# Attention with value blocks of two score chunks instead of three, and row-maximum groups issued in pairs at every second block

## The chip, the cores and the metric

The kernel runs on one core of a Trainium2 chip. The metric is the time of one execution on the device in microseconds (us); a time of the kernel is the median of several executions. Engines are named as the profile names them: PE is the TensorE matmul, PEld its weight loads, DVE VectorE, ACT ScalarE, POOL GpSimd and SP SyncE, which here only issues transfers.

## What is computed

One transformer block with adaptive layer norm, on x of shape (2, 2048, 256), in float32:

```python
h = _layernorm(x, axis=-1) * (1 + ca) + sa
x = x + ga * _L0_attn_ref(h, ...)
h = _layernorm(x, axis=-1) * (1 + cb) + sb
x = x + gb * _L0_ffn_ref(h, ...)
```

The attention has 16 heads of size 16. With q = (h W_q + b_q) W_s, k = h W_k + b_k and v = h W_v + b_v, it is softmax(q k^T / 4) v for every head, followed by W_o and b_o. The feed-forward part is a router with 8 experts, each of which takes its best 512 tokens. The change touches only the attention.

## The kernel before

**Stages.** The projections of q, k and v come first (to some 130 us), then the attention loop (to some 1396 us), then the residual and second norm, the selection of tokens, and the experts. All engines run their own programs and meet at semaphores.

**The attention's units.** There are 2 x 16 heads and each is cut into two halves of 1024 queries: 64 units (`UNITS`). A unit has 16 key tiles of 128 (`KT`). For a unit the kernel does three things on PE:

- *Row-maximum groups.* A group (`fill_group`, matmuls on L223) computes scores of 128 queries against 1024 keys into two PSUM banks, with two matmuls of 512 columns, one in the upper 64 rows of the array and one in the lower. DVE reduces each group to maxima (`reduce_group`, L230). A unit has 16 groups. There are two slots of two banks, and `next_group(n)` waits on L1120 until group n - 2 has been reduced. After the first group of the next unit is reduced, DVE joins the 16 results (`join_maxima`, L241 and L247), POOL splits them into a high and a low part (`split_maxima`), and SP carries them through DRAM (L200, then L205) into two extra rows of the queries' operand.
- *Score chunks.* `scores(pe, s, half)` (one matmul of 512 columns on L584) computes 128 keys by 512 queries, with the maximum already subtracted by the extra rows. A unit has 32 chunks. They go through three banks (`SCORE_BANKS`): chunk n waits until chunk n - 3 has been read. ACT takes the exponential of each chunk (L1080) into `pt`. Even chunks use the upper rows of the array and odd ones the lower. The first chunk of a unit waits for the maxima to have landed (L576).
- *Value blocks.* `weigh(block)` multiplies the exponentials of a block of chunks by the values (L1139), into `acc` in bank 7. The output uses 32 columns of the array for each quarter of the queries, so four matmuls run side by side. Each one is float32 and appears as two records. A block waits for its exponentials, and the unit's first block also for ACT to have copied the previous unit's output.

**The order on PE** is written by hand in the loop from L1149. Each round issues the value block that lies `DELAY` = 2 rounds back, then the next score chunks, with groups between them. With `BLOCK` = 3 a unit of 32 chunks has `BLOCKS` = 11 value blocks: a first one of two chunks (`FIRST_BLOCK`) and ten of three. A three-chunk block has eight matmuls: four of 256 columns and four of 128. Every round issues three chunks, or two where b == DELAY, and one or two groups, 16 in the 11 rounds of a unit. Groups run ahead of the scores by some 24 key tiles, so they end before the scores do.

**The order on ACT** is that of the chunks. Before one chunk of each unit it copies the output of the unit before, after all of that unit's value blocks are done:

```python
for n in range(STEPS * 2):
    if n % UNIT_CHUNKS == BLOCK and n > UNIT_CHUNKS:
        take_output(n // UNIT_CHUNKS - 1)
```

where `take_output(u)` waits for `pv_done` of (u + 1) * BLOCKS and makes the copy on L1066. These lines are 1068 to 1070.

**The order on SP** is, for each unit: store the output that ACT has copied, carry the next unit's maxima (`place_maxima`), bring the output into its place, and, after a head's second unit, load the operands of a head to come (`load_next`, twelve transfers, after all scores of the head are issued).

Of the kernel before, what the change touches and what calls it, by code (L numbers as in the profile page):

```python
# [46 lines left out]
UNITS = G * HALVES  # L47
STEPS = UNITS * KT
# [3 lines left out]
AHEAD = KT + LEAD  # L52
EARLY = 3
EARLY_GROUPS = 25
BLOCK = 3
DELAY = 2
UNIT_CHUNKS = 2 * KT
BLOCKS = -(-UNIT_CHUNKS // BLOCK)
FIRST_BLOCK = UNIT_CHUNKS - (BLOCKS - 1) * BLOCK
QB = CH // 4  # L60
# [33 lines left out]
def adaln_moe_block(nc, x, w_q, b_q, w_k, b_k, w_v, b_v, w_o, b_o, w_s, router_w, router_b,  # L94
                    w1, b1, w2, b2, c, w_mod, out):
    ctx = ExitStack()
    with ctx:
# [19 lines left out]
        def bank(i, n=1):  # L117
            return ps[:, i * 512:(i + n) * 512]
# [98 lines left out]
        def fill_group(pe, n, slot):  # L217
            u, k = divmod(n, KT)
            h, f = divmod(u, HALVES)
            r, a, c = h % NBUF, f * (QT // 2) + k // NCH, k % NCH  # L220
            for half in range(2):
                rows = slice(HALF * half, HALF * half + KROWS)
                last = nc.tensor.matmul(slot[:, half * CH:(half + 1) * CH], qp[rows, r, a * P:(a + 1) * P],  # L223
                                        kp[rows, r, c * CH:(c + 1) * CH], start=True, stop=True)
            last.then_inc(groups_full, 1)
# [345 lines left out]
        def scores(pe, s, half):  # L571
            u, kt = divmod(s, KT)
            h, f = divmod(u, HALVES)
            n = s * 2 + half
            if kt == 0 and half == 0:
                pe.wait_ge(maxima_in[u % 2], (u // 2 + 1) * 32)  # L576
            if n == 0:
                pe.wait_ge(minus_in, 16 * 2 * NBUF)
            if n == 2:
                pe.wait_ge(low_done, chunks * 4 - 1)  # L580
            if n >= SCORE_BANKS:
                pe.wait_ge(scores_out, n - SCORE_BANKS + 1)
            rows = slice(HALF * half, HALF * half + MROWS)
            nc.tensor.matmul(bank(n % SCORE_BANKS), kp[rows, h % NBUF, kt * P:(kt + 1) * P],  # L584
                             qp[rows, h % NBUF, f * CH:(f + 1) * CH], start=True, stop=True).then_inc(scores_full, 1)
# [249 lines left out]
        def project_rows(pe, n):  # L835
            if n == 0:
                pe.wait_ge(xb_ready, 2 * NB)
                pe.wait_ge(groups_out, STEPS)
                pe.wait_ge(normalised, G // HG // NB * HALVES)
            if n >= NCH and n % 2 == 0:  # L840
                pe.wait_ge(normalised, (G // HG - 1) * HALVES + (n - NCH) // 2 + 1)
            for half in range(2):
                if n > 0:
                    pe.wait_ge(y_out, n * 2 + half - 1)
                for t in range(2):
                    at = (n % NCH) * CH + (half * 2 + t) * P
                    for k in range(KD):
                        last = nc.tensor.matmul(y_bank(half)[:, t * D:(t + 1) * D], ao[:, n // NCH * KD + k, at:at + P],
                                                wog[:, n // NCH, k, :], start=k == 0, stop=k == KD - 1)
                last.then_inc(y_full, 1)  # L850
# [41 lines left out]
        with nc.Block() as block:  # L892
# [9 lines left out]
            def blocks_until(n):  # L902
                u, c = divmod(n, UNIT_CHUNKS)
                return u * BLOCKS + (c - FIRST_BLOCK) // BLOCK + 2

            def chunks_of(block):
                u, b = divmod(block, BLOCKS)
                end = u * UNIT_CHUNKS + FIRST_BLOCK + b * BLOCK
                return range(end - (BLOCK if b else FIRST_BLOCK), end)

            def group_slot(n):
                return bank(5 - 2 * (n % 2), 2)
# [147 lines left out]
            def _(act):  # L1060
                project_act(act)
                def take_output(u):
                    act.wait_ge(pv_done, (u + 1) * BLOCKS)
                    if u > 1:
                        act.wait_ge(o_stored[u % 2], (u // 2) * 16)
                    nc.scalar.copy(o_sb[:, u % 2, :], acc).then_inc(acc_out, 1)  # L1066
# [4 lines that stand above are left out]
# [35 lines left out]
            @block.tensor  # L1106
            def _(pe):
                project_pe(pe)
                mm = nc.tensor.matmul

                def next_group(n):
                    u, k = divmod(n, KT)
                    h, f = divmod(u, HALVES)
                    r = h % NBUF
                    if f == 0 and k == 0:
                        pe.wait_ge(operands_in[r], (h // NBUF + (r > 0)) * 16 * loads_of_head)
                    if n == EARLY_GROUPS:
                        pe.wait_ge(low_done, chunks * 4)
                        pe.wait_ge(v_out, chunks * 2 - 1)
                    pe.wait_ge(groups_out, n - 1)  # L1120
                    fill_group(pe, n, group_slot(n))

                def weigh(block):
                    u, b = divmod(block, BLOCKS)
                    h = u // HALVES
                    if b == 0:
                        pe.wait_ge(v_staged, h + 1)
                        pe.wait_ge(v_out, chunks * 2)
                        if u > 0:
                            pe.wait_ge(acc_out, u)  # L1130
                    ready = chunks_of(block)
                    pe.wait_ge(scores_out, ready[-1] + 1)
                    for s in sorted({n // 2 for n in ready}):
                        kt = s % KT
                        halves = [n % 2 for n in ready if n // 2 == s]
                        first, many = halves[0], len(halves)
                        probs = pt[:, s % PTS, first * CH:(first + many) * CH].rearrange("p (h t) -> p h t", h=many)
                        for j in range(4):
                            last = mm(acc[32 * j:32 * (j + 1), first * QB:(first + many) * QB], v_st[:, h % NBUF, kt, :],  # L1139
                                      probs[:, :, j * QB:(j + 1) * QB], start=kt == 0, stop=kt == KT - 1)  # L1140
                    last.then_inc(pv_done, 1)

                next_group(EARLY_GROUPS)
                for s in range(1, EARLY):
                    for half in range(2):
                        scores(pe, s, half)
                blocks = UNITS * BLOCKS
                group, chunk = EARLY_GROUPS + 1, 2 * EARLY
                for block in range(DELAY, blocks):  # L1149
                    weigh(block - DELAY)  # L1150
                    b = block % BLOCKS
                    many = FIRST_BLOCK if b == DELAY else BLOCK
                    twice = b != DELAY and (b == 0 or b > DELAY and b % 2 == 1) or block == 2 * DELAY
                    for n in range(many):
                        if n == (0 if twice or b == DELAY else 1) and group < STEPS:
                            next_group(group)
                            group += 1
                        scores(pe, *divmod(chunk, 2))
                        chunk += 1
                    if twice and group < STEPS:  # L1160
                        next_group(group)
                        group += 1
                    if block == blocks - DELAY:
                        project_rows(pe, 0)
                for block in range(blocks - DELAY, blocks):
                    weigh(block)
                post_pe(pe)
# [629 lines left out]
```

## Time and profile before

| what | value |
|---|---|
| median of 3 runs | 1736.73 us (1732.57 to 1737.1) |
| profiled execution | 1736.54 us |
| its span (first to last instruction) | 1734.7 us |
| granted TensorE clock, mean | 0.979 |
| attention loop in it | some 139 to 1396 us |
| instructions | 43731 |

The span is what the profile divides into shares; the execution's own time is 1.8 us longer. A group of instructions is one line of the kernel on one engine with one operation. "Busy" is time in which at least one of the group runs, and "idle before" is time in which the engine had nothing just before them, with what ended it. In a timeline, instructions of one line that follow each other are merged, with their count; the first number is the start of the first one in us and the second is the time until the last one ends. Ends of matmuls are modelled and overlap the next start, so costs on PE are read from start to start.

### The profile page before, as it was taken

Reading aid. Unit: us, or ns where it says so; the run is one execution under the profiler, and the core shown is the slowest. Engines: PE = TensorE matmul, PEld = TensorE weight load, DVE = VectorE, ACT = ScalarE, POOL = GpSimd, SP = SyncE. Lnnn points to the kernel's source line nnn. Section 1 sums busy time; section 2 is a strip of 40 time slices with the busy share of each in tenths; the row PEclk is TensorE's granted clock in tenths of the full one; section 3 lists DMA queues with packets and bytes.
Section 4 is the critical chain, followed back from the end, with each engine's and each line's share of the span. In section 5 each row is a group of like instructions: output and inputs, shape, how many; then the busy total and the mean of one; then the engine's idle time right before and its main releaser. Section 6 shows DMA issues by size and latency. Waiting matters only on the chain. (4 is left out here: it accounts for less than half of the span.)

```text
span 1734.7 us, 43731 instructions
## 1 busy us (share of the span) xinstructions
PE 1685.5 (97%) x17251; PEld 969.8 (56%) x17251; DVE 1513.5 (87%) x1908; ACT 1291.7 (74%) x2454; POOL 229.3 (13%) x300
## 2 busy tenths in 40 slices
PE   8999999999999999999999999999999998599998
PEld 5645555555555555555555554555555586488887
DVE  5678999999999999999999999999999476687774
ACT  2327888888888888888888888888888834365663
POOL 0422012100010000001000000100000012135433
PEclk9999999999999999999999999999999997599999
DMA  8660443222222223323222223342220331235332
GB/s 265 207 178 24 92 98 53 41 41 39 52 55 39 41 49 52 47 40 65 41 42 39 39 41 54 59 60 39 41 42 12 108 107 61 98 101 143 89 82 37
DMA packets 93658, 122.03 MB, mean 70 GB/s; under 512 B 24060, under 2 KB 70716, under 8 KB 90348
## 3 DMA queue, kind: packets, MB, share of 16 engines
q1 hardware_dynamic: 84492, 109.22, 28.1%
q0 software_dynamic: 6144, 8.39, 2.7%
q8 instruction: 136, 2.23, 0.6%
q10 hardware_dynamic: 2816, 1.61, 0.3%
q14 instruction: 70, 0.57, 0.1%
HBM read 79.35 MB, written 38.54 MB: 68 GB/s over the span
## 5 line engine op out<-in xcount | busy, mean ns | idle before, releaser
L230 DVE TENSOR_REDUCE pmax<-ps 128x2 f32<-128x1024 f32 x1024 | 1191.6, 1215 | 54.2 <-PE ps L223 50.2
L1080 ACT ACTIVATE pt<-ps 128x512 f32<-128x512 f32 x2048 | 1079.4, 600 | 179.8 <-PE ps L584 157.7
L223 PE MATMUL ps<-kp,qp 48*128 48x512 f32 x2048 | 622.4, 458 | 2.9 <-DVE pmax L230 2.9
L1139 PE MATMUL ps<-pt,v_st 128*32 128x256 f32 (+1 forms) x10752 | 589.7, 334 | 0.7 <-ACT pt L1080 0.7
L584 PE MATMUL ps<-qp,kp 50*128 50x512 f32 x2048 | 560.8, 422 | 0.5 <-ACT pt L1080 0.5
L584 PEld LDWEIGHTS ps<-qp,kp 50*128 50x128 f32 x2048 | 292.5, 185 | 265.2 <-ACT pt L1080 263.1
L1139 PEld LDWEIGHTS ps<-pt,v_st 128*32 128x32 f32 x10752 | 265.7, 109 | 261.0 <-issue 187.2
L223 PEld LDWEIGHTS ps<-kp,qp 48*128 48x128 f32 x2048 | 245.6, 184 | 108.1 <-issue 89.8
L213 POOL CAST m_parts<-rowmax_t 128x32 fp32r<-128x32 f32 x64 | 13.5, 211 | 864.5 <-DVE rowmax_t L247 864.5
L1752 PE MATMUL ps<-w_l,hid_h 128*128 128x256 f32 x256 | 72.3, 283 | 0.0
L446 ACT ACTIVATE pt<-ps,xb 128x512 fp32r<-128x512 f32 x32 | 21.8, 687 | 64.7 <-PE ps L613 63.7
L1518 POOL DMA_INDIRECT y<-b_row,scatter_at x32 | 59.0, 1843 | 35.4 <-DVE b_row L1641 29.0
L613 PE MATMUL ps<-pt,xb 128*128 128x512 f32 x128 | 59.1, 603 | 0.0
L1508 POOL DMA_INDIRECT stage_a<-h_rows,gather_at x32 | 39.0, 1218 | 129.3 <-DVE gather_at L1618 122.0
L1752 PEld LDWEIGHTS ps<-w_l,hid_h 128*128 128x128 f32 x256 | 48.9, 191 | 0.0
L1007 POOL COPY v_st<-v_all 128x256 f32<-128x256 f32 x32 | 12.6, 398 | 260.5 <-PE ps L1139 260.5
L1734 PE MATMUL ps<-qp,kp 128*128 128x512 f32 x128 | 44.3, 428 | 1.4 <-ACT qp L1536 1.2
L1734 PE MATMUL ps<-qp,w_l 128*128 128x512 f32 x128 | 40.2, 396 | 0.0
L1734 PE MATMUL ps<-kp 128*128 128x512 f32 x128 | 40.1, 394 | 0.0
L1536 ACT CAST qp<-ps 128x512 fp32r<-128x512 f32 x16 | 8.6, 590 | 42.0 <-PE ps L1706 42.0
L543 DVE SCALAR_TENSOR_TENSOR pt<-ps,xb,pt 128x512 f32<-128x512 f32 x32 | 23.7, 746 | 17.3 <-ACT pt L446 17.2
L613 PEld LDWEIGHTS ps<-pt,xb 128*128 128x128 f32 x128 | 23.2, 189 | 26.0 <-issue 24.5
(229 smaller groups left out, 1297.6 us busy)
## 6 DMA issues: line engine op xcount, KB each, us to landing
kp<-k_parts SPq DMA_DIRECT2D x186, 128.0 KB, 4.5
v_all<-L_ffn_w SPq DMA_DIRECT2D x16, 1024.0 KB, 6.9
qp<-q_parts SPq DMA_DIRECT2D x186, 64.0 KB, 4.1
k_parts<-pt SPq DMA_DIRECT2D x16, 512.0 KB, 3.4
q_parts<-pt SPq DMA_DIRECT2D x16, 512.0 KB, 2.9
o_rows<-o_sb SPq DMA_DIRECT2D x64, 128.0 KB, 3.4
sums_c<-o_rows SPq DMA_DIRECT2D x512, 0.5 KB
m_rows<-m_parts SPq DMA_DIRECT2D x256, 2.0 KB
```

What stands on the lines that cost most here:

```text
L223: last = nc.tensor.matmul(slot[:, half * CH:(half + 1) * CH], qp[rows, r, a * P:(a + 1) * P], kp[rows, r, c * CH:(c + 1) * CH], start=True ...
L230: v.reduce_max(pmax[:, u % 2, 2 * k:2 * k + 2], slot.rearrange("p (f t) -> p f t", f=2), AX.X).then_inc(groups_out, 1)
L446: nc.scalar.activation(parts[u][:, 0].bitcast(F32R), unit_bank(n, u), ACT.Identity, bias=unit_bias(u)).then_inc(high_done, 1)
L543: v.scalar_tensor_tensor(parts[u][:, 1], unit_bank(n, u), unit_bias(u), parts[u][:, 0], ALU.add, ALU.subtract).then_inc(low_done, 1)
L584: nc.tensor.matmul(bank(n % SCORE_BANKS), kp[rows, h % NBUF, kt * P:(kt + 1) * P], qp[rows, h % NBUF, f * CH:(f + 1) * CH], start=True, st ...
L613: last = mm(unit_bank(n, u), w[:, k, (u % 2) * P:(u % 2 + 1) * P], h_t[n % 2][:, k, :], start=k == 0, stop=k == KD - 1)
L1080: nc.scalar.activation(pt[:, s % PTS, half * CH:(half + 1) * CH], bank(n % SCORE_BANKS), ACT.Exp, scale=SCALE).then_inc(scores_out, 1)
L1139: last = mm(acc[32 * j:32 * (j + 1), first * QB:(first + many) * QB], v_st[:, h % NBUF, kt, :], probs[:, :, j * QB:(j + 1) * QB], start=kt ...
L1508: nc.gpsimd.indirect_dma_start(tok_rows[:, e % 2, cc, :], None, h2_dram, bass.IndirectOffsetOnAxis(ap=gather_at[:, e % 2, cc:cc + 1], axis ...
L1518: nc.gpsimd.indirect_dma_start(out_flat, bass.IndirectOffsetOnAxis(ap=scatter_at[:, e % 2, cc:cc + 1], axis=0), contrib[:, cc, :], None, c ...
L1734: last = mm(bank(2 + f % 2), w[:, k, f * P:(f + 1) * P], t[:, k, :], start=i + k == 0, stop=i + k == KD + 1)
L1752: last = mm(eo_tile(at), h[:, f, tok], w[:, f, :], start=False, stop=f + i == NF + 1)
```

## The change

`BLOCK` goes from 3 to 2. By the formulas that stay, a unit then has `BLOCKS` = 16 value blocks of two chunks, all alike, with four matmuls of 256 columns each. The loop on PE issues one score chunk more before it begins. Each round then issues one value block and two chunks. Rounds with an even number (`pair`) also issue two groups, one before the chunks and one after them; rounds with an odd number issue none. The copy of the output on ACT, whose place is given by `BLOCK`, comes before the third chunk of a unit instead of the fourth.

```diff
--- before.py
+++ after.py
@@ -52,7 +52,7 @@
 AHEAD = KT + LEAD
 EARLY = 3
 EARLY_GROUPS = 25
-BLOCK = 3
+BLOCK = 2
 DELAY = 2
 UNIT_CHUNKS = 2 * KT
 BLOCKS = -(-UNIT_CHUNKS // BLOCK)
@@ -1146,18 +1146,18 @@
                         scores(pe, s, half)
                 blocks = UNITS * BLOCKS
                 group, chunk = EARLY_GROUPS + 1, 2 * EARLY
+                scores(pe, *divmod(chunk, 2))
+                chunk += 1
                 for block in range(DELAY, blocks):
                     weigh(block - DELAY)
-                    b = block % BLOCKS
-                    many = FIRST_BLOCK if b == DELAY else BLOCK
-                    twice = b != DELAY and (b == 0 or b > DELAY and b % 2 == 1) or block == 2 * DELAY
-                    for n in range(many):
-                        if n == (0 if twice or b == DELAY else 1) and group < STEPS:
+                    pair = block % 2 == 0
+                    for n in range(min(BLOCK, UNITS * UNIT_CHUNKS - chunk)):
+                        if n == 0 and pair and group < STEPS:
                             next_group(group)
                             group += 1
                         scores(pe, *divmod(chunk, 2))
                         chunk += 1
-                    if twice and group < STEPS:
+                    if pair and group < STEPS:
                         next_group(group)
                         group += 1
                     if block == blocks - DELAY:
```

## Rows read from the trace of the kernel before

**Rows 1.** The page, part 1: busy us of each engine, share of span, instructions.

```profile
PE 1685.5 (97%) x17251; PEld 969.8 (56%) x17251; DVE 1513.5 (87%) x1908; ACT 1291.7 (74%) x2454; POOL 229.3 (13%) x300
```

**Rows 2.** Instructions grouped by line, 300 to 1300 us: busy, mean ns | idle before.

```profile
L230 DVE TENSOR_REDUCE pmax<-ps 128x2 f32<-128x1024 f32 x815 | 946.9, 1214 | 37.5 <-PE ps L223 34.4
L1080 ACT ACTIVATE pt<-ps 128x512 f32<-128x512 f32 x1629 | 858.9, 600 | 134.5 <-PE ps L584 116.3
L223 PE MATMUL ps<-kp,qp 48*128 48x512 f32 x1628 | 497.7, 457 | 0.5 <-DVE pmax L230 0.5
L1139 PE MATMUL ps<-pt,v_st 128*32 128x256 f32 (+1 forms) x8552 | 469.0, 334 | 0.0
L584 PE MATMUL ps<-qp,kp 50*128 50x512 f32 x1630 | 444.5, 421 | 0.0
L584 PEld LDWEIGHTS ps<-qp,kp 50*128 50x128 f32 x1628 | 232.3, 185 | 210.2 <-ACT pt L1080 210.2
```

**Rows 3.** Line 1066, 300 to 1300 us: count, ns min/median/max, first and last start.

```profile
L1066 ACT COPY o_sb<-ps x51: 389/391/392, 316.4 to 1299.1; 128x256 f32<-128x256 f32 x51
```

**Rows 4.** Timeline of PE, 805 to 812 us: start, us, engine, line, count.

```profile
808.02 0.64 PE L1139 MATMUL ps<-pt,v_st 128*32 128x256 f32 x8
808.59 0.50 PE L223 MATMUL ps<-kp,qp 48*128 48x512 f32 x2
808.93 0.40 PE L584 MATMUL ps<-qp,kp 50*128 50x512 f32 x2
809.26 0.86 PE L1139 MATMUL ps<-pt,v_st 128*32 128x256 f32 x16
```

**Rows 5.** Timeline of PE, 812 to 827 us.

```profile
812.00 0.50 PE L584 MATMUL ps<-qp,kp 50*128 50x512 f32 x1
...
812.34 0.39 PE L584 MATMUL ps<-qp,kp 50*128 50x512 f32 x1
...
812.58 0.41 PE L584 MATMUL ps<-qp,kp 50*128 50x512 f32 x1
812.92 0.86 PE L1139 MATMUL ps<-pt,v_st 128*32 128x256 f32 x16
813.71 0.50 PE L223 MATMUL ps<-kp,qp 48*128 48x512 f32 x2
...
814.89 0.86 PE L1139 MATMUL ps<-pt,v_st 128*32 128x128 f32 x16
815.67 0.50 PE L584 MATMUL ps<-qp,kp 50*128 50x512 f32 x1
...
816.59 0.86 PE L1139 MATMUL ps<-pt,v_st 128*32 128x256 f32 x16
...
825.07 0.66 PE L584 MATMUL ps<-qp,kp 50*128 50x512 f32 x3
```

**Rows 6.** Timeline of DVE, 812 to 824 us.

```profile
816.52 0.18 DVE L241 TENSOR_REDUCE rowmax<-pmax 128x8 f32<-128x32 f32 x1
...
816.87 4.57 DVE L230 TENSOR_REDUCE pmax<-ps 128x2 f32<-128x1024 f32 x4
```

**Rows 7.** Timeline of ACT, 804 to 813 us.

```profile
803.97 1.57 ACT L1080 ACTIVATE pt<-ps 128x512 f32<-128x512 f32 x3
...
807.38 0.39 ACT L1066 COPY o_sb<-ps 128x256 f32<-128x256 f32 x1
807.65 1.60 ACT L1080 ACTIVATE pt<-ps 128x512 f32<-128x512 f32 x3
809.41 1.09 ACT L1080 ACTIVATE pt<-ps 128x512 f32<-128x512 f32 x2 [0.16 <-PE ps L584]
```

**Rows 8.** Timeline of ACT and PEld, 812.5 to 815 us.

```profile
812.60 1.57 ACT L1080 ACTIVATE pt<-ps 128x512 f32<-128x512 f32 x3 [0.15 <-PE ps L584]
...
814.22 0.18 PEld L584 LDWEIGHTS ps<-qp,kp 50*128 50x128 f32 x1 [0.22 <-ACT pt L1080]
```

**Rows 9.** Timeline of PE, 1362 to 1394 us, where the groups have ended.

```profile
1365.26 0.86 PE L1139 MATMUL ps<-pt,v_st 128*32 128x128 f32 x16
...
1367.20 0.86 PE L1139 MATMUL ps<-pt,v_st 128*32 128x256 f32 x16
...
1370.64 0.86 PE L1139 MATMUL ps<-pt,v_st 128*32 128x256 f32 x16
...
1390.59 3.72 PE L848 MATMUL ps<-wog,ao 128*128 128x256 f32 x16
```

**Rows 10.** Timeline of DVE and SP, 834 to 842 us.

```profile
836.16 0.18 DVE L241 TENSOR_REDUCE rowmax<-pmax 128x8 f32<-128x32 f32 x1
...
837.22 1.30 SPq L200 DMA_DIRECT2D m_rows<-m_parts  x4
...
839.42 0.53 SPq L205 DMA_DIRECT2D qp<-m_rows  x2
```

**Rows 11.** Timeline of SP, 816 to 823 us.

```profile
822.35 0.53 SPq L205 DMA_DIRECT2D qp<-m_rows  x2
```

## The prediction

> **What bounds the kernel now.** Four fifths of the span is the attention loop. I read the page first: TensorE (PE) is busy 97%, VectorE (DVE) 87%, ScalarE (ACT) 74% [rows 1]; three engines close to full, so averages do not decide. The grouped rows of the loop's middle say who waits: DVE's reductions sat idle 37.5 us in 1000, nearly all for PE; ACT 134.5 us, for PE; PE's weight loads wait on ACT for 210 us, yet PE has no idle time of its own [rows 2]. One unit (16 groups, 32 score chunks, one output copy) takes (1299.1 - 316.4)/50 = 19.65 us [rows 3].
>
> The timelines then show whether PE is continuous. I measure from the start of one piece to the start of the next. A value block of three chunks holds PE 0.79 us (812.92 to 813.71), the unit's short block of two chunks 0.57 (808.02 to 808.59) [rows 4, 5]. Between value blocks lie 1.18 us with two groups and three chunks (813.71 to 814.89), 0.92 with one group and three chunks (815.67 to 816.59), and 0.67 after the short block (808.59 to 809.26). A unit has 10, 1, 5, 5 and 1 of them: 7.90 + 0.57 + 5.90 + 4.60 + 0.67 = 19.64. That is the whole unit: **PE's issue order is the bound**, and a pause of PE is paid in full. DVE's floor is lower: its reductions start 1.13 us apart when they run back to back (4.57 us for four, the last one 1.22 long [rows 6]), 16 x 1.13 = 18.1 a unit, plus 0.35 for the joining of maxima (816.52 to 816.87) [rows 6]: 18.45.
>
> **Inside a block** the two row halves run together, so matmuls go in slots of two. A slot costs 0.24 (812.34 to 812.58), but the first after a value block 0.34 (808.59 to 808.93, 812.00 to 812.34) and the last before one 0.33 (808.93 to 809.26) [rows 4, 5]. So each edge of a value block costs some 0.10 us, and there will be 16 blocks a unit in place of 11. The Trainium skill ("TensorEngine Tiling (Array Packing)", Key Properties) says that changing the tiling mode drains the array; the value blocks use 32-column tiles and the others do not, so this rule speaks against the change, and the trace agrees with it.
>
> **The change, part by part, against a unit of 19.65.**
> 1. Value blocks: 16 of two chunks at 0.57 = 9.12 (before 8.47): **+0.65**. The same columns are streamed; what is saved is only the third chunk's passes of half width.
> 2. Even blocks: group, two scores, group = three full slots, 0.34 + 0.24 + 0.33, measured 0.92 in the blocks with three slots. Odd blocks: two scores, one slot that has both edges, 0.43: three slots take 0.92 and two 0.67, so one more or less is 0.24 or 0.25. No row shows a slot alone between value blocks; its bounds are 0.33 (one edge free) and 0.50 (the second half late by 0.06, since its bank comes free just then: the score three chunks earlier starts 1.13 earlier, and takes 0.48 to ACT (808.93 to 809.41 [rows 4, 7]), 0.60 there and 0.05 back (814.17 to 814.22 [rows 8])). I take 0.43, nearest to the measured edges. Sum 8 x (0.92 + 0.43) = 10.80 (before 11.17): **-0.37**; full slots are the gain here.
> 3. A pair of blocks is then 0.57 + 0.92 + 0.57 + 0.43 = 2.49 with two groups; DVE needs 2.26. So the DVE gaps grow, and it hides behind PE. Once a unit, the join makes the next reduction start 0.35 late, and the second group of the next even block, whose slot is the one just being read, comes some **0.25** late. Before, DVE was behind by more and PE never waited there.
> 4. **The copy of the output (L1066).** ACT makes it before the exponential of chunk n with n % 32 == BLOCK: third chunk of a unit after, fourth before. It waits for the unit's last value block. After the change this block is issued in iteration 16U+1, behind score chunk 32U+4, and that score waits (three banks) for the exponential of chunk 32U+1. So when ACT has made chunk 32U+1 and comes to the copy, the value block that it wants has by program order not begun. Before, only chunk 32U+2 had to be issued, for which the exponential of 32U-1 is enough: ACT has three exponentials in hand, and the copy starts without idle time (807.38, right behind an exponential [rows 7]). Worked out from the even block's first group at 0: scores 0.34, second group 0.58, last value block 0.91; its matmuls take 0.64 [rows 4] and 0.08 pass to ACT (score ending 809.33, exponential 809.41 [rows 4, 7]): copy at 1.63; exponential 32U+2 at 1.90 (copy to next, 807.38 to 807.65 [rows 7]), ends 2.50. PE meanwhile finished the value block at 1.48 and wants score 32U+5, which waits for exactly this exponential: it starts at 2.55 [rows 8]. Score 32U+6 waits for the next exponential (1.90 + 0.49 + 0.60, spacing from 1.57 us for three [rows 7]), 3.05; the next value block follows 0.34 later at 3.39 and not at 1.91. **+1.48** per unit, 63 times. Behind this wait are queued, on PE, the next value block and the next groups, so DVE starves too; nothing there has slack with which to make it up. Its floor is the wait for the first of these scores alone, 2.55 - 1.48 = 1.07.
>
> Unit: 9.12 + 10.80 + 0.25 + 1.48 = **21.65**, or +2.00. Groups last from block 2 to 998, 997/16 = 62.3 units: +124.6 us. The tail of scores without groups goes by ACT and the three banks: now 3.44 us for six chunks (1367.20 to 1370.64 [rows 9]), 24 blocks at about 1.10 (0.33 + 0.57 + the 0.20 that a bank comes late) = 26.4 for the 25.3 of now (1365.26 to 1390.59), and one more copy: +2.5. One chunk more ahead of the loop waits for an exponential: +0.5. What follows the attention stays: +127.6 in all. The profiled execution took 1736.54, the median of the three runs is 1736.73, no difference, so I forecast **1864 us**.
>
> Costed at nothing: the smaller number of value matmuls (their issue is within the 0.57), the pt slots (twelve chunks, and the values stay within eight of ACT), and **the row maxima**. These must land before a unit's first score. Now this score starts 8.55 us after the join (816.52 to 825.07 [rows 5, 6]); after, groups lead by three pairs of blocks, 7.47 + 0.34 + 0.25 - 1.67 = 6.4 (the score follows the block's first group by 0.34, the join by 0.54 + 1.13). The save is issued 1.06 after the join, the load 3.27 (836.16, 837.22, 839.42 [rows 10]), its second part ends at 3.8; the save, as small, was seen landed 0.9 after its last issue ended (838.52 to 839.42), so the load is there at about 5. That holds, with some 1.4 to spare. In a few units the load comes 5.83 after the join (822.35 [rows 11]), because the next head's operands were still in the queues; those are started at a unit's end, which moves away from the next join by over 3 us.
>
> **The rivals.**
> (a) *Edges are hidden.* The odd blocks' slot costs its lower bound 0.33, the pair is 2.39, and the unit 19.12 + 0.25 + 1.48 = 20.85, +1.20: 1736.5 + 74.8 + 3 = **1814**. Against it: every edge in [rows 4, 5] costs its 0.10. The Trainium skill ("TensorE: Matmul & The Clock Gate", Step-by-step) lets weight loads be pulled ahead of matmuls in flight, which would do this; at these edges the trace disagrees. 0.13.
> (b) *The maxima come late.* If the load lands 1.5 us later than worked out in most units, PE waits 0.5 to 1 us at L584 with everything behind it: +0.7 x 62.3 = 44, **1908**. For it: the collisions of [rows 11]; against: their cause moves away. 0.09.
> (c) *Not slower.* The bound passes to DVE at L230: PE's pieces shrink so far that the unit is DVE's 18.45 (the edges on both sides of the even blocks gone as well: 16 x 0.20 = 3.2 is more than is asked), and the copy costs its floor of 1.07: 19.52, -0.13 x 62.3 + 3: **1731**. It decides only if PE's 32 pieces a unit take under 19.65 - 1.07 = 18.58 together; the rows give 19.92. 0.03.
> (d) *The copy isn't late.* If the wait at the copy cost nothing, the rest would be 20.17, +0.52 x 62.3 + 2: **1771**. Program order speaks against it. 0.05.
>
> **How the numbers follow.** Forecast 0.70; its own range is 1825 (odd slot 0.37, no 0.25 at the join, some of the copy's wait made up) to 1893 (odd slot at its bound of 0.50, +0.56 a unit, and less elsewhere). (a) 0.13, (b) 0.09, (d) 0.05, (c) 0.03. The range of 8 in 10 goes from 1810, which takes in (a), to 1893; (b), (c) and (d) lie outside. A measurement of this kernel tells 0.3% from nothing (5 us). Faster by over that 0.03, within it 0.02, slower 0.95.
>
> **What would show it.** Copies 21.65 us apart; ACT idle about 1.4 us before each of 63 copies, put down to PE L1139, where it had none; PE's weight load L584 waiting for ACT over 1 us once a unit; blocks of 0.57; pairs of blocks 2.49 apart, the single slot 0.43; DVE idle in total over 180 us, for PE. The prediction is wrong if copies still start right behind an exponential, or if pairs of blocks come at 2.3.

## The result and the profile after

| kernel | median | runs | ratio to before (95% interval) | granted TensorE clock in the profiled execution |
|---|---|---|---|---|
| before | 1735.64 us | 4, 1732.57 to 1737.1 | | 0.979 |
| changed | 2306.63 us | 4, 2237.15 to 2397.17 | 1.2987 (1.2822 to 1.3153) | 0.712 |

The changed kernel is slower, as forecast, but by 571 us and not by 128. The ratio is taken from the two shorter executions of the changed kernel alone, because the other two lie over 1.5% above the shortest; by those two it is 518 us slower, by the median of all four 571. The four runs lie up to 7% apart, which no run of the kernel before does, and the longer the run, the lower its granted clock: 2237 us at 0.781, 2270 at 0.767, 2343 at 0.734, 2397 at 0.712. The profiled execution is the last of these.

The page of the changed kernel, parts 1 and 2. The digits are the 40 slices of the span; PEclk is the granted clock in tenths.

```profile
PE 2283.6 (95%) x14691; PEld 1020.1 (43%) x14691; DVE 1529.8 (64%) x1908; ACT 1327.1 (55%) x2454; POOL 229.6 (10%) x300
...
PE   8999999999999999999999999999999999978998
...
PEclk9975655755589768655585576559866755868999
```

PE is busy for 2284 us where it was busy for 1686, though it has 2560 fewer matmuls ([rows 1] is the same line of before). PEclk says why. In the attention nearly every slice stands between 5 and 8 tenths, where the kernel before had 9 from the second slice to the 33rd. Two neighbouring windows show what is behind these means. The columns are the busy us and counts of PE, PEld, DVE, ACT and POOL, then the granted clock, the DMA share and GB/s:

```profile
590.49:672.41 81.92, 79.94 (x444) 28.00 (x442) 44.86 (x43) 40.61 (x76) 1.32 (x5) 0.50 0.13 22
672.41:709.96 37.55, 35.47 (x330) 15.42 (x328) 31.90 (x32) 29.67 (x56) 3.71 (x6) 1.00 0.15 38
```

The clock is 0.50 or 1.00, that is 1.2 or 2.4 GHz, and it changes every few units. In its own records the attention, from the first copy to the last but one, lies at 0.50 for 1259 of 1858 us.

The groups of the page that answer to [rows 2]. The columns are the same, but over the whole span:

```profile
L230 DVE TENSOR_REDUCE pmax<-ps 128x2 f32<-128x1024 f32 x1024 | 1207.9, 1217 | 682.8 <-PE ps L223 672.7
L1080 ACT ACTIVATE pt<-ps 128x512 f32<-128x512 f32 x2048 | 1106.6, 597 | 677.3 <-PE ps L584 664.5
L1139 PE MATMUL ps<-pt,v_st 128*32 128x256 f32 x8192 | 920.3, 534 | 0.0
L584 PE MATMUL ps<-qp,kp 50*128 50x512 f32 x2048 | 651.1, 600 | 63.0 <-ACT pt L1080 63.0
L223 PE MATMUL ps<-kp,qp 48*128 48x512 f32 x2048 | 614.7, 596 | 3.2 <-DVE pmax L230 2.2
L584 PEld LDWEIGHTS ps<-qp,kp 50*128 50x128 f32 x2048 | 300.7, 254 | 428.3 <-ACT pt L1080 428.1
...
L1066 ACT COPY o_sb<-ps 128x256 f32<-128x256 f32 x64 | 23.8, 372 | 120.7 <-PE ps L1139 120.7
```

The mean matmul of L1139 went from 334 to 534 ns; part of this is that all of them now have 256 columns. DVE and ACT are each idle some 675 us, both for PE. The copy on L1066, which had no idle time before it, now has 120.7 us, put down to PE L1139: 1.9 us for each.

**At full clock the unit is the predicted one.** The copies of two units, one stretch at each level:

```profile
L1066 ACT COPY o_sb<-ps x2: 372/372/373, 621.9 to 658.0; 128x256 f32<-128x256 f32 x2
...
L1066 ACT COPY o_sb<-ps x2: 372/372/373, 685.3 to 707.0; 128x256 f32<-128x256 f32 x2
```

A unit takes 21.7 us at 2.4 GHz (685.29 to 707.02 in the timeline below, 21.73; forecast 21.65) and 36.1 us at 1.2 GHz. The timeline of PE around a copy in a stretch at full clock:

```profile
684.58 0.64 PE L1139 MATMUL ps<-pt,v_st 128*32 128x256 f32 x8
686.21 0.99 PE L584 MATMUL ps<-qp,kp 50*128 50x512 f32 x2 [0.99 <-ACT pt L1080]
687.13 0.64 PE L1139 MATMUL ps<-pt,v_st 128*32 128x256 f32 x8
...
689.17 0.50 PE L584 MATMUL ps<-qp,kp 50*128 50x512 f32 x2
689.60 0.64 PE L1139 MATMUL ps<-pt,v_st 128*32 128x256 f32 x8
690.17 0.50 PE L223 MATMUL ps<-kp,qp 48*128 48x512 f32 x2
```

The timeline of ACT there, with the next unit's copy:

```profile
685.29 0.37 ACT L1066 COPY o_sb<-ps 128x256 f32<-128x256 f32 x1 [1.43 <-PE ps L1139]
685.56 2.56 ACT L1080 ACTIVATE pt<-ps 128x512 f32<-128x512 f32 x5
...
707.02 0.37 ACT L1066 COPY o_sb<-ps 128x256 f32<-128x256 f32 x1 [1.42 <-PE ps L1139]
```

The last value block of the unit starts at 684.58, and the score behind it at 686.21 instead of 685.15: 1.63 us, worked out as 1.64. PE's own record is of 0.99 us idle. ACT is idle 1.43 us ahead of the copy. A lone slot between value blocks takes 0.43 (689.17 to 689.60), as taken, and a value block 0.57 (689.60 to 690.17). So the working of the blocks and of the pause holds. Whether the excess is all the clock's is what run 3 below tests.

In a stretch at half clock PE's pieces are nearly twice as long, and PE's idle time in the pause is what it was (timeline of PE):

```profile
656.89 1.08 PE L1139 MATMUL ps<-pt,v_st 128*32 128x256 f32 x8
658.96 1.28 PE L584 MATMUL ps<-qp,kp 50*128 50x512 f32 x2 [0.99 <-ACT pt L1080]
660.17 1.08 PE L1139 MATMUL ps<-pt,v_st 128*32 128x256 f32 x8
661.18 0.79 PE L223 MATMUL ps<-kp,qp 48*128 48x512 f32 x2
```

A value block takes 1.01 (660.17 to 661.18), against 0.57. The idle time before the score is again 0.99.

One low stretch of the attention does not follow a copy at all: it goes from 139.9 to 163.8, ahead of the first copy at 168.9, and PE is busy for all of its 23.90 us. Before it lies the stop of 0.51 us with which the loop begins (138.24).

### The profile page after: what moved, and what is told of

Its sections match the earlier page's. It is cut to its first block and busy times, and to the rows that moved or that the text cites. A ratio compares the mean times of both kernels' runs of the same rounds, so it can differ in the third digit from the quotient of the medians.

```text
span 2395.4 us, 38611 instructions
## 1 busy us (share of the span) xinstructions
PE 2283.6 (95%) x14691; PEld 1020.1 (43%) x14691; DVE 1529.8 (64%) x1908; ACT 1327.1 (55%) x2454; POOL 229.6 (10%) x300
## 5 line engine op out<-in xcount | busy, mean ns | idle before, releaser
L230 DVE TENSOR_REDUCE pmax<-ps 128x2 f32<-128x1024 f32 x1024 | 1207.9, 1217 | 682.8 <-PE ps L223 672.7
L1080 ACT ACTIVATE pt<-ps 128x512 f32<-128x512 f32 x2048 | 1106.6, 597 | 677.3 <-PE ps L584 664.5
L1139 PE MATMUL ps<-pt,v_st 128*32 128x256 f32 x8192 | 920.3, 534 | 0.0
L584 PE MATMUL ps<-qp,kp 50*128 50x512 f32 x2048 | 651.1, 600 | 63.0 <-ACT pt L1080 63.0
L584 PEld LDWEIGHTS ps<-qp,kp 50*128 50x128 f32 x2048 | 300.7, 254 | 428.3 <-ACT pt L1080 428.1
L223 PEld LDWEIGHTS ps<-kp,qp 48*128 48x128 f32 x2048 | 260.5, 252 | 375.9 <-issue 283.0
L1139 PEld LDWEIGHTS ps<-pt,v_st 128*32 128x32 f32 x8192 | 186.4, 126 | 438.9 <-issue 358.9
L1066 ACT COPY o_sb<-ps 128x256 f32<-128x256 f32 x64 | 23.8, 372 | 120.7 <-PE ps L1139 120.7
L789 DVE TENSOR_TENSOR xb<-ps,xb 128x512 f32<-128x512 f32 x16 | 10.5, 680 | 47.0 <-PE ps L848 47.0
L1610 DVE TENSOR_TENSOR stage_b<-lane,col_row 128x1024 bf16<-128x1024 bf16 x32 | 37.2, 1221 | 0.3
```

Source lines behind the costliest of these rows:

```text
L230: v.reduce_max(pmax[:, u % 2, 2 * k:2 * k + 2], slot.rearrange("p (f t) -> p f t", f=2), AX.X).then_inc(groups_out, 1)
L1080: nc.scalar.activation(pt[:, s % PTS, half * CH:(half + 1) * CH], bank(n % SCORE_BANKS), ACT.Exp, scale=SCALE).then_inc(scores_out, 1)
L1610: v.tensor_tensor(one_hot[:, g8 % 2], lane[:, n, g8 * 8:(g8 + 1) * 8].unsqueeze(2).broadcast_to([P, 8, P]), col_row[:].unsqueeze(1).broadc ...
```

## The experiments

Theory A was: the copy stops PE once a unit, and through these pauses the granted clock falls. Its rival, theory B: the new pattern of blocks lets it fall, pause or not. All medians are of four runs, beside runs of the kernel before on the same chip, whose medians are 1735.68 to 1736.36 us. Runs 1 to 4 were made on one chip, 5 to 8 on a second and 9 to 11 on a third.

**1. The copy two chunks later.**

```diff
-                    if n % UNIT_CHUNKS == BLOCK and n > UNIT_CHUNKS:
+                    if n % UNIT_CHUNKS == BLOCK + 2 and n > UNIT_CHUNKS:
```

> Edit to the changed kernel: ACT copies the output before the fifth chunk of a unit, not the third. Theory A (the copy that stands too early stops PE for 1.07 us and then 0.5 us once a unit, and it is these pauses that make the granted clock of TensorE fall to 0.5 for whole stretches; the rest of the change costs only 0.5 us a unit): the pauses are gone but for some 0.1 us, the clock stays at 1.0 through the attention, copies are some 20.1 us apart, and the time is near 1771 us (1755 to 1785). Theory B (it is the new pattern of blocks itself, with single slots and more edges, that lets the clock fall, pause or not): the clock still falls to 0.5 in stretches and the time stays above 2000 us.

Measured: 1791.77 us, ratio 1.0354 (1.0295 to 1.0413), clock 0.981. From the first copy on, no stretch of the attention is at 0.5. Moving one instruction of ACT takes 515 us off the changed kernel. The time is 21 us over what was expected; the timeline of PE, at a join and at a copy, shows where it is:

```profile
645.32 0.40 PE L584 MATMUL ps<-qp,kp 50*128 50x512 f32 x2
645.77 0.50 PE L223 MATMUL ps<-kp,qp 48*128 48x512 f32 x2
...
654.25 0.50 PE L584 MATMUL ps<-qp,kp 50*128 50x512 f32 x2
655.01 0.64 PE L1139 MATMUL ps<-pt,v_st 128*32 128x256 f32 x8 [0.26 <-ACT o_sb L1066]
```

The lone slot before the unit's first value block lasts 0.76 (654.25 to 655.01), not 0.43, because this block waits for the copy, which ACT begins only at 654.39 (timeline of ACT):

```profile
654.39 0.37 ACT L1066 COPY o_sb<-ps 128x256 f32<-128x256 f32 x1 [0.18 <-PE ps L1139]
```

That is 0.33 a unit, 20 us. The delay by the join is there too: its second group starts 0.45 behind the scores (645.32 to 645.77), not 0.24, so 0.21 where 0.25 was forecast.

**2. The pause in the kernel before.**

```diff
-                    if n % UNIT_CHUNKS == BLOCK and n > UNIT_CHUNKS:
+                    if n % UNIT_CHUNKS == 0 and n > 0:
```

> Edit to the kernel before: ACT copies the output before the first chunk of a unit, not the fourth; blocks of three as they were. By program order the last value block has then not begun when ACT comes to the copy, as in the changed kernel. Theory A: a pause of some 1.1 us and shorter ones behind it once a unit; at full clock that is about 1.7 us a unit and 1843 us, but the clock falls as in the changed kernel and the time is 2100 to 2400 us. Theory B: the pause costs only itself, the clock stays at 1.0, 1830 to 1860 us.

Measured: 1953.93 us (1931.38 to 2003.75), clock 0.916. The early copy alone, with blocks of three as they were, stops PE by the same 0.99 us (timeline of PE):

```profile
727.02 0.86 PE L1139 MATMUL ps<-pt,v_st 128*32 128x128 f32 x16
728.87 0.49 PE L584 MATMUL ps<-qp,kp 50*128 50x512 f32 x1 [0.99 <-ACT pt L1080]
```

and brings the clock down in stretches (the page's row of the granted clock):

```profile
PEclk9999655599999999999999999999999989689999
```

It is less than the 2100 to 2400 us expected. The profile has one long stretch at 0.5 (five units of 35.6 us, slices 5 to 8, some 72 us lost) and then only short ones, one in every third unit. At full clock its units are 21.13 us. The pause is enough to make the clock fall; how often it falls depends on something else too.

**3. The pause of the changed kernel, filled.** PE repeats a group that it has made, into the slot of the one that comes next.

```diff
                     weigh(block - DELAY)
+                    if block > BLOCKS and block % BLOCKS == 1 and group < STEPS:
+                        pe.wait_ge(groups_out, group - 1)
+                        for _ in range(3):
...
+                            for half in range(2):
...
+                                mm(group_slot(group)[:, half * CH:(half + 1) * CH], qp[rows, r, at * P:(at + 1) * P],
+                                   kp[rows, r, c * CH:(c + 1) * CH], start=True, stop=True)
```

> Edit to the changed kernel: behind each unit's last value block PE repeats three times a row-maximum group that it has already made, into the slot of the group that comes next (which is then filled as before), so that it has work in most of the pause while ACT still comes late. It starts when that slot is free, some 0.3 us into the pause, and takes 0.8 us. Theory A: ACT waits at the copy as before, but PE sits idle for 0.3 us and less at a time, the clock stays at 1.0 (or falls rarely), copies are 21.7 to 22.0 us apart and the time is 1865 to 1890 us, against 2300 without the filler. Theory B: no gain, or slower by the added work: 2300 us or more.

Measured: 1867.39 us, ratio 1.0768 (1.0731 to 1.0804), clock 0.982. This is the run that decides. Work that nobody needs, 372 matmuls of it, makes the kernel 439 us faster. The timeline of PE around the copy:

```profile
658.03 0.64 PE L1139 MATMUL ps<-pt,v_st 128*32 128x256 f32 x8
658.94 0.96 PE L1161 MATMUL ps<-kp,qp 48*128 48x512 f32 x6 [0.27 <-DVE pmax L230]
659.75 0.90 PE L584 MATMUL ps<-qp,kp 50*128 50x512 f32 x2
660.58 0.64 PE L1139 MATMUL ps<-pt,v_st 128*32 128x256 f32 x8
```

The copy in the timeline of ACT:

```profile
658.74 0.37 ACT L1066 COPY o_sb<-ps 128x256 f32<-128x256 f32 x1 [1.43 <-PE ps L1139]
```

Two windows of the attention (columns as above, the clock third from the end):

```profile
500.00:800.00 300.00, 295.32 (x2734) 130.10 (x2736) 262.32 (x248) 242.03 (x456) 13.60 (x35) 1.00 0.26 43
800.00:1100.00 300.00, 295.20 (x2734) 129.91 (x2732) 262.99 (x252) 242.02 (x456) 14.08 (x37) 1.00 0.25 43
```

ACT waits 1.43 us at the copy as before, the unit takes 21.74 us as before, and the next value block comes as late as before (658.03 to 660.58, 2.55; in the changed kernel 684.58 to 687.13, 2.55). Only PE is different: it has the added matmuls, its idle time is 0.27 us, and the clock stays at 1.00. So 1867 us is the changed kernel's time without its loss of clock. The forecast for that was 1864.

**4. Without the chunk ahead of the loop.**

```diff
-                scores(pe, *divmod(chunk, 2))
-                chunk += 1
                 for block in range(DELAY, blocks):
```

> Edit to the changed kernel: the one score chunk that was issued ahead of the loop is left out, so that each round's value block stands one chunk earlier against the scores; the copy stays before the third chunk. Theory A: the last value block begins one exponential earlier, so ACT's wait and PE's first pause shrink by 0.5 us, from 1.07 to about 0.6 us; at full clock a unit takes some 21.2 us. If the clock answers to the length of the pause it falls less often: 1835 us with no fall, up to 2200 with some. Theory B: no less falling of the clock than in the changed kernel, 2250 us and more.

Measured: 1830.94 us, ratio 1.0544 (1.0519 to 1.0569), clock 0.981. Copies are 21.19 us apart, and PE's idle time is 0.56 us (timeline of PE):

```profile
688.73 0.50 PE L584 MATMUL ps<-qp,kp 50*128 50x512 f32 x1
689.80 0.49 PE L584 MATMUL ps<-qp,kp 50*128 50x512 f32 x1 [0.56 <-ACT pt L1080]
```

No stretch of the attention is at 0.5. The added chunk, which should give PE more lead, is what lengthens the pause from 0.56 to 0.99: it puts the last value block behind one more exponential.

**5. The copy one chunk later.**

```diff
-                    if n % UNIT_CHUNKS == BLOCK and n > UNIT_CHUNKS:
+                    if n % UNIT_CHUNKS == BLOCK + 1 and n > UNIT_CHUNKS:
```

> Edit to the changed kernel: the copy stands before the fourth chunk, not the third, so that the first of PE's two stopped scores is issued at once and only the second waits for the copy. By the same working as for the unit of 21.65: second score at 2.55, value block at 2.88 instead of 1.91, a unit of some 21.1 us, and one pause in which PE's records show 0.6 us of idle time where the changed kernel shows 0.99. Theory A1 (a pause of 0.57 us, as in the run without the lead chunk, leaves the clock alone; one of 0.99 does not): clock 1.0 in the attention, 1825 to 1840 us. Theory A2 (what counts is a stall of the scores at this place, whatever its length): stretches at 0.5 and over 1900 us.

Measured: 1837.95 us, ratio 1.0608 (1.0575 to 1.0642), clock 0.974. Copies are 21.25 us apart, PE is idle 0.56 us, and as long as there are groups the clock stays at 1.0, as expected. The profiled execution (1849.66 us, the longest of the four) was at 0.5 for 24 us near the attention's end (1481 to 1505), where the scores run without groups.

**6. One group in every round**, with the copy before the fifth chunk.

```diff
-                    pair = block % 2 == 0
...
-                        if n == 0 and pair and group < STEPS:
+                        if n == 0 and group < STEPS:
...
-                    if pair and group < STEPS:
-                        next_group(group)
-                        group += 1
```

> Edit to the changed kernel: blocks of two, but one group in every round ahead of its two scores, in place of two in every second round; the copy stands before the fifth chunk. A round is a value block of 0.57 and two slots of 0.67 together: 16 x 1.24 = 19.84 us a unit; the copy fits between the exponentials of chunks four and five and is done before the next unit's first value block, and the join delays no group. If the slots and edges are all there is, copies are 19.85 to 19.95 us apart and the time is 1748 to 1756 us, against 1792 with pairs and the same copy. If pairs cost nothing of their own, the time stays at 1785 to 1795 us.

Measured: 1762.45 us (1760.77 to 1778.45), ratio 1.018 (1.0138 to 1.0223), clock 0.979. It is 29 us under the same kernel with pairs, so pairs do have a price: PE's waits at the join and at the copy are gone. A unit takes (1285.1 - 643.8)/32 = 20.04 us in the mean, 19.99 in the median, and not 19.84 (timeline of PE):

```profile
658.08 0.64 PE L1139 MATMUL ps<-pt,v_st 128*32 128x256 f32 x8
...
659.32 0.64 PE L1139 MATMUL ps<-pt,v_st 128*32 128x256 f32 x8
...
660.60 0.64 PE L1139 MATMUL ps<-pt,v_st 128*32 128x256 f32 x8
```

Rounds take 1.24 (658.08 to 659.32) to 1.28 (659.32 to 660.60), and this scatter makes most of the missing 0.2. This is the fastest kernel with blocks of two, and it is 27 us slower than blocks of three.

Its profile also shows a fall of the clock without any stop at a copy. One unit's first score waited 2.31 us for the maxima, and from 520.1 to 523.5 us the clock was at 0.5 (timeline of PE, and a window with the columns as above):

```profile
518.78 0.50 PE L584 MATMUL ps<-qp,kp 50*128 50x512 f32 x1 [2.31 <-DMA qp<-m_rows]
...
520.10:523.50 3.40, 3.40 (x24) 0.90 (x20) 2.22 (x2) 1.60 (x3) 0.00 (x0) 0.50 0.00 1
```

Three more scores waited for the maxima, 0.26 to 0.38 us each, and no fall followed. With single groups the maxima are at times late, as the prediction's rival (b) has it, though in few units.

**7. A pause of 0.76 us.** To the kernel of run 4 is added, behind the output's copy:

```diff
                         take_output(n // UNIT_CHUNKS - 1)
+                        nc.scalar.copy(spare[:], ident[:])
```

> Edit to the kernel without the lead chunk (1831 us, PE idle 0.57 us once a unit, clock 1.0): ACT makes one more small copy (128 columns, into a tile that nothing reads) right behind the copy of the output, which lengthens PE's pause by some 0.17 us to about 0.74. At full clock the unit grows by the same 0.17 us: some 1842 us. If the clock falls already at this length, stretches at 0.5 appear and the time is over 1880 us; theory A1 gives no side between 0.57 and 0.99, I expect no fall (0.6).

Measured: 1928.66 us (1873.87 to 1974.04), clock 0.964 in the profiled execution, which is the shortest. PE's idle time is 0.76 to 0.77 us (timeline of PE; L585 is the score chunk's line here), a unit at full clock 21.39:

```profile
659.72 0.49 PE L585 MATMUL ps<-qp,kp 50*128 50x512 f32 x1 [0.77 <-ACT pt L1082]
```

The clock does fall, which I had held less likely: 0.2 us more of ACT's time a unit, 12 us in all, cost some 98 us in the median and 43 in the shortest execution. (Run 4 was made on another chip; no run tells what that contributes.)

**8. One group in every round, with the early copy** (the edit of run 6 without the later copy).

> Edit to the changed kernel: one group in every round as in the run with single groups, with the copy left before the third chunk as the change has it. PE now has a group to issue while ACT waits, so the pause is shorter: idle 0.5 to 0.7 us in the records in place of 0.99. Unit 19.84 + 1.25 = 21.1 us at full clock; theory A1: clock 1.0 in the attention and 1825 to 1840 us. If the early copy by itself brings the falls, whatever PE has to do, the time is over 1900 us.

Measured: 1948.16 us, ratio 1.1147 (1.1117 to 1.1177), clock 0.907. A miss. PE's idle time is as expected, and as in runs 4 and 5 (timeline of PE):

```profile
712.23 0.49 PE L223 MATMUL ps<-kp,qp 48*128 48x512 f32 x2
713.29 0.99 PE L584 MATMUL ps<-qp,kp 50*128 50x512 f32 x2 [0.57 <-ACT pt L1080]
```

and yet the clock falls (the page's row):

```profile
PEclk9998869989989988998976998999589969679999
```

So the longest idle piece of a unit does not by itself tell whether the clock stays.

**9. The pause filled once** (run 3 with `range(1)` for `range(3)`).

> As the run with the pause filled, but the spare group is issued once, not three times: it starts when its slot is free, some 0.3 us into the pause, runs 0.34 us, and leaves a second idle piece of about 0.2 us. Theory C (the clock falls because PE stands idle in one piece of 0.75 us or more; two short pieces in its place are harmless): clock 1.0 in the attention, copies 21.7 us apart, 1862 to 1875 us. Theory D (the sum of idle time in a unit counts, or something else of the block's pattern): some falls, over 1890 us.

Measured: 2020.57 us (1946.89 to 2041.29), clock 0.886. Theory C falls. PE is idle in two pieces of 0.27 and 0.22 us (timeline of PE):

```profile
697.00 0.50 PE L1161 MATMUL ps<-kp,qp 48*128 48x512 f32 x2 [0.27 <-DVE pmax L230]
697.72 0.99 PE L584 MATMUL ps<-qp,kp 50*128 50x512 f32 x2 [0.22 <-ACT pt L1080]
```

That is less in all than the 0.56 us of run 4, which kept its clock. One spare group wins 286 us, the next two another 153.

**10. Run 8 with one spare group in the pause.**

```diff
                             next_group(group)
                             group += 1
+                            if block > BLOCKS and block % BLOCKS == 1 and group < STEPS:
+                                pe.wait_ge(groups_out, group - 1)
...
```

> Edit to the run with single groups and the early copy (1948 us, PE idle 0.56 us once a unit, and yet stretches at 0.5): one spare group behind the real one in the pause. If it is still the pause by which that kernel's clock falls, the falls go and the time is 1830 to 1850 us. If the pattern of single groups lets the clock fall by itself, stretches at 0.5 stay and the time is over 1900 us; the run with single groups and no pause (1762 us, one fall of 3.4 us in its profile) speaks against that.

Measured: 1848.42 us, ratio 1.064 (1.058 to 1.07), clock 0.976. With its pause filled, run 8 gets its clock back; the units stay 21.20 us long. So there too it was the pause. Its profile lost clock only ahead of the first copy, up to 160 us. Four of its first scores waited for the maxima by over 0.3 us, the longest 0.66, and no fall followed.

**11. A shorter pause in the kernel before.**

```diff
-                    if n % UNIT_CHUNKS == BLOCK and n > UNIT_CHUNKS:
+                    if n % UNIT_CHUNKS == 1 and n > UNIT_CHUNKS:
```

> Edit to the kernel before, blocks of three: the copy stands before the second chunk of a unit, so ACT has one exponential in hand when it comes to wait, and PE's pause is some 0.5 us shorter than with the copy before the first chunk (idle 0.99 us there, 1954 us). Idle about 0.5 to 0.6 us. Theory C: clock 1.0 in the attention; at full clock the unit is some 20.6 us, 1790 to 1805 us. If the clock falls already here, over 1830 us.

Measured: 1830.48 us, ratio 1.0555 (1.0485 to 1.0625), clock 0.961. PE is idle 0.32 us a unit (timeline of PE), the unit takes 20.65 us, and yet the clock fell twice in the profiled execution, for 37.5 us each time, and each time two units took 56.8 us together and not 41.3. The second line is the window of the first fall:

```profile
692.05 0.98 PE L584 MATMUL ps<-qp,kp 50*128 50x512 f32 x2 [0.32 <-ACT pt L1080]
...
472.25:509.79 37.54, 37.54 (x254) 18.20 (x252) 21.63 (x21) 18.27 (x35) 2.83 (x3) 0.50 0.20 36
```

Inside that window PE has no idle time at all in its records, although a copy lies in it (502.94), and the clock stays at 0.50. So a low stretch does not need the pause to last. At full clock alone it would be 1736 + 1.0 x 62.3 = 1798 us, and 31 more come from the two falls. Another miss of theory C.

All of them in one table. Unit is the distance of copies at full clock, idle the time that PE's records show at the stop, clock the mean over the profiled execution, which is 0.98 where the attention loses next to none:

| kernel | unit, us | PE idle, us | clock | median, us |
|---|---|---|---|---|
| before | 19.65 | none at a copy | 0.979 | 1736 |
| 6 single groups, copy at fifth | 20.04 | none at a copy | 0.979 | 1762 |
| 1 copy at fifth | 20.53 | 0.26 | 0.981 | 1792 |
| 11 before, copy at second | 20.65 | 0.32 | 0.961 | 1830 |
| 4 no chunk ahead | 21.19 | 0.56 | 0.981 | 1831 |
| 5 copy at fourth | 21.25 | 0.56 | 0.974 | 1838 |
| 10 run 8 filled | 21.20 | none over 0.15 in most units | 0.976 | 1848 |
| 3 filled by three | 21.74 | 0.27 | 0.982 | 1867 |
| 7 run 4, longer pause | 21.39 | 0.76 | 0.964 | 1929 |
| 8 single groups, early copy | 21.24 | 0.57 | 0.907 | 1948 |
| 2 before, early copy | 21.13 | 0.99 | 0.916 | 1954 |
| 9 filled by one | 21.74 | 0.27 + 0.22 | 0.886 | 2021 |
| changed | 21.73 | 0.99 | 0.712 | 2307 |

From its first copy on, the attention of the kernel before has a single stop, ahead of a group at 1082.98, and the clock stays at 1.0 behind it (timeline of PE):

```profile
1082.98 0.50 PE L223 MATMUL ps<-kp,qp 48*128 48x512 f32 x2 [0.54 <-DVE pmax L230]
```

## Why the prediction was wrong

**Its sign and its mechanism held; the size did not.** The whole is +571 us. The runs divide it: blocks of two as such, +27 (run 6 against before); pairs of groups, with the waits that they bring at the join and the copy, +29 (run 1 against 6); the copy standing too early, at full clock, +76 (run 3 against 1); the loss of clock, **+439** (the changed kernel against run 3, in medians; +386 by its two shorter executions). The first three make +132, for which the sum had +127.6. Between themselves they do not divide as the prediction has it, since in run 1 the copy still costs 20 us: counted against a copy that costs nothing it is 76 + 20 = 96, for which the sum had 62.3 x 1.48 = 92.

Step by step:

- *Steps 1 and 2, the pieces of the blocks*: right. 0.57 and 0.43 were measured; the slot that no row of before showed lay at the value taken, so rival (a) is refuted.
- *Step 3, the join*: 0.21 for 0.25, measured in run 1. Right.
- *Step 4, the copy*: right in place and size. 1.63 for 1.64 to the first score, 2.55 for 2.48 (3.39 - 0.91) to the next value block, once a unit.
- *The sum*: "Unit: ... = 21.65", measured 21.73 at full clock.
- **The step that failed** is the sentence that "**a pause of PE is paid in full**" and no more, and with it the whole of the sum's durations, which were all taken from rows at full clock. I priced what the pause delays, and never asked what clock the rest of the unit would then be granted. Each of PE's pieces was taken as 0.57, 0.92 or 0.43 for all 62 units, and for two thirds of the attention a value block was 1.01, and a unit that lay wholly at half clock took 36.1 us. The pause is paid in full and more than that in the clock: 1.48 us a unit was priced, and the loss of clock came to 439 us on top. The range had no case for it. The trace of before shows that the clock can fall, behind the attention, in a window where PE was busy for 30.12 us of 50:

```profile
1450.00:1500.00 50.00, 30.12 (x150) 21.94 (x148) 35.72 (x181) 24.00 (x54) 10.08 (x24) 0.53 0.25 85
```

The stops there are as long as 3 us, and behind the one stop of 0.54 us in the attention nothing fell. So that trace was reason to keep a case for the lower clock, and no more; it did not show that a regular stop of 1 us would do it.
- *The maxima* came in time, as costed: the second transfer was issued 3.26 us after the join in the median and at most 5.04 (before: 3.27, 5.84). The head's loads did move away from the join. Rival (b) did not happen in the changed kernel.
- *Rivals (c) and (d)*: not seen; ACT was idle 1.43 us at the copy, and a unit of 19.52 was not near in any run.
- *A slip*: the attention is 1257 of 1735 us, under three quarters of the span and not four fifths. No sum uses it.

What the prediction named as signs was nearly all there (pieces of 0.57, the slot of 0.43, ACT idle 1.43 us before each copy, PE idle about 1 us), and would not have told of the larger cost. The sign to look at was the one that it left out, the PEclk line.

**Shown** is that with the pause the clock falls again and again (the changed kernel, 2, 8), that without it the attention keeps its clock (1), and that filling it brings the clock back with the schedule otherwise unchanged (3, 10). Spare matmuls take away idle time and add work, and no run puts them at another place; run 1, which adds no work, is the one that speaks for the idle time. **Open** is what about a pause decides. Not its longest piece: 0.56 us fell in run 8 and not in 4 and 5. Not the idle sum of a unit: 0.49 fell in run 9, 0.32 in run 11, 0.56 not in run 4. I know of no number in these records that orders the thirteen kernels. The repeats of one kernel also differ (2237 to 2397 us, 1874 to 1974 us), so part of it is not in the program at all. The stop of 0.51 us at the start of the loop shows the same: in the changed kernel 24 us at half clock follow it, in runs 1 and 3, which have it too, none. How much depends on the chip was not tested, but 5, 7 and 8, which differ, ran on one.

## What to carry to other kernels

Where PE has been continuous, a new stop of even half a microsecond at a regular place can cost several times its length, because PE's work behind it may be granted half the clock. It need not: run 8 lost clock with 0.57 us, runs 4 and 5 kept it with 0.56. Before pricing such a stop, work out the unit at both levels and keep a case for the lower one in the range. If a stop cannot be removed, test it with spare matmuls in it: that separates its own price (here 76 us) from the clock's (439 us), and it wins back the clock's part.

When the size of a block changes, look for every place that uses the same constant as a position. Here `BLOCK` also placed a copy on ACT, and moving that one copy by two chunks was worth 515 us. No version here with blocks of two beat the kernel before. It may be that blocks of three fit the three score banks, each score waiting for its own place one round ago; no run changed the banks, so this is not shown.

## What the runs showed of the hardware

- TensorE was granted half its clock in an attention where it was never idle for more than 0.99 us at a time; it was busy for 79.94 of 81.92 us in the window at 0.50 above. The Trainium skill ("TensorE: Matmul & The Clock Gate", Why this matters for your kernels) advises against idle gaps between bursts of matmuls, and the gaps that it names there are longer than any stop in this attention. In this case the runs decide against reading that as a safe limit.
- At half clock a unit took 36.11 us against 21.73. The matmuls' pieces grew by 1.7 to 1.8 (a value block from 0.57 to 1.01), and ACT's exponentials and DVE's reductions did not change (597 and 1217 ns in the mean, against 600 and 1214 in [rows 2]).
- A low stretch could last long, 82 us in that window and 181 in run 2 (206.8 to 387.7), with the same short pause once a unit that stretches at full clock had as well. It could also last with no pause in it: 23.9 us in the changed kernel and 37.54 in run 11, PE busy throughout. So continuous work did not bring the clock back at once.
- Single stops, not repeated at the same place in every unit, had a fall behind them or not: 2.31 us in run 6 did, 0.54 in the kernel before and up to 0.66 in run 10 did not.
- A spare group was free where PE was waiting anyway: with three in each pause, the unit stayed within 0.01 us (21.74 against 21.73).
